# A vision transformer layer with routed experts on one core: end of the attention pipeline, choice of experts and residual traffic rearranged

## The reference

```python
h = einsum('bnd,de->bne', patches(x), W)                  # 768 -> 192
h = h + attention(layernorm(h))                           # 12 heads of 16, causal over 36 tokens
logits = layernorm(h) @ router_w.T                        # 8 experts
probs = softmax(logits); top_w, top_i = top_k(probs, 2); top_w /= top_w.sum()
for e in range(8):
    out += w_e * (gelu(flat @ w1[e] + b1[e]) @ w2[e] + b2[e])   # 192 -> 768 -> 192
h = h + out
```

## Time and profile before

| | |
|---|---|
| median of 3 runs | 444.54 us (441.53 to 458.2) |
| profiled execution | 444.34 us |
| its span | 442.4 us |
| mean granted TensorE clock | 0.903 |
| instructions | 14569 |

### The profile page before, as it was taken

How to read it: one execution, slowest core, us unless ns; L and a number is a source line. 1 busy time by engine, 2 the same in 40 slices (tenths; PEclk the granted TensorE clock), 3 DMA queues, 4 the chain that set the end, 5 groups by cost and what they waited for, 6 DMA issues and landing times.

```text
span 442.4 us, 14569 instructions
## 1 busy us (share of the span) xinstructions
PE 354.8 (80%) x5602; PEld 329.0 (74%) x5602; DVE 253.1 (57%) x638; ACT 219.8 (50%) x451; POOL 194.4 (44%) x236
## 2 busy tenths in 40 slices
PE   2788879998989899987622279799899898999920
PEld 2687779888989889877512169799899898999920
DVE  2566447787787766765349734455455455455417
ACT  3555648778888687753411024344344444344400
POOL 9005433446756664332630144465455455454220
PEclk9899999999999999975555579999999999999985
DMA  8757001444432333311006026621111111122039
GB/s 310 212 153 225 3 17 23 122 124 121 120 111 52 98 92 110 107 46 43 3 2 167 5 51 192 218 64 57 46 57 55 55 57 55 48 57 56 28 140 368
DMA packets 28654, 42.81 MB, mean 97 GB/s; under 512 B 12261, under 2 KB 18901, under 8 KB 28461
## 3 DMA queue, kind: packets, MB, share of 16 engines
q1 hardware_dynamic: 24460, 33.37, 25.0%
q0 software_dynamic: 4128, 8.50, 6.6%
HBM read 30.23 MB, written 9.67 MB: 90 GB/s over the span
## 4 chain that ended last, share of the span: by engine, by line
PE 45%; DVE 15%; issue 14%; POOL 10%; ACT 8%; DMA 6%; SPq 1%; POOLq 0%; DVEq 0%; ACTq 0%
PE PSA L1177 16%; PE PSA L1192 13%; PE PSA L958 4%; POOL XF L438 3%; POOL YP L450 2%; DMA REG<-xrows,KBR 2%; DMA W2l<-wqkv 2%; PE PSA L1015 2%; DVE H L947 2%; DVE REG L652 2%; PE PSA L1196 2%; PE PSA L1144 2%; DVE PTR L880 1%; PE PSA L990 1%; PE PSA L1041 1%
## 5 line engine op out<-in xcount | busy, mean ns | idle before, releaser
L1177 PE MATMUL PSA<-YT,W1h 128*128 128x128 f16 x774 | 79.4, 221 | 6.4 <-issue 4.7
L1177 PE MATMUL PSA<-YT,W1l 128*128 128x128 f16 (+1 forms) x516 | 76.6, 222 | 0.0
L482 POOL DMA_INDIRECT yrows<-KBR x43 | 43.9, 1022 | 69.0 <-DVE KBR L924 68.7
L1177 PEld LDWEIGHTS PSA<-YT,W1h 128*128 x774 | 64.6, 99 | 10.8 <-issue 5.5
L1192 PE MATMUL PSA<-W2h,PTR 128*128 x516 | 71.0, 246 | 0.3 <-DVE PTR L652 0.3
L638 ACT ACTIVATE PTR<-PSA 128x768 f32<-128x768 f32 x43 | 34.9, 811 | 69.3 <-PE PSA L1177 69.3
L1192 PE MATMUL PSA<-W2l,PTR 128*128 x258 | 63.5, 246 | 0.0
L477 POOL DMA_INDIRECT REG<-xrows,KBR x43 | 42.5, 987 | 43.0 <-DVE KBR L901 25.3
L643 ACT ACTIVATE PTR<-PTR 128x768 f16<-128x768 f32 x43 | 36.3, 843 | 46.2 <-PE PSA L1196 46.1
L652 DVE SCALAR_TENSOR_TENSOR PTR<-PTR 128x768 f16<-128x768 f32 x43 | 41.2, 958 | 25.9 <-ACT PTR L643 25.9
L958 PE MATMUL PSA<-W2h,REG 128*108 128x192 f16 x396 | 39.2, 261 | 17.7 <-DVE REG L652 17.6
(11 more groups left out here) (163 smaller groups left out, 794.6 us busy)
## 6 DMA issues: line engine op xcount, KB each, us to landing
WSTG<-w SPq DMA_DIRECT2D x16, 384.0 KB, 3.8
WSTG<-w SPq DMA_DIRECT2D x16, 336.0 KB, 3.2
REG<-xt SPq DMA_DIRECT2D x12, 324.0 KB, 4.5
W1l<-xt SPq DMA_DIRECT2D x10, 324.0 KB, 3.4
VB<-VP SPq DMA_DIRECT2D x99, 19.1 KB
hrows<-H SPq DMA_DIRECT2D x1, 1782.0 KB
H<-hrows SPq DMA_DIRECT2D x1, 1728.0 KB, 8.0
xrows<-REG SPq DMA_DIRECT2D x1, 1600.5 KB
```

The costliest lines, as they stand in the source:

```text
L482: gp.indirect_dma_start(out=yrows, out_offset=bass.IndirectOffsetOnAxis(ap=TARGET[:, s:s + 1], axis=0), in_=YO[s % 2], in_offset=None).the ...
L1177: ins = nc.tensor.matmul(bank(2 * u + f // (FC // 2), 128, FC // 2 * ST_)[:, w:w + ST_], weights[a, c], YT[0:rows, at:at + ST_], start=k = ...
```

## The change

- The loop of steps ends at step 21. What is left is written out by hand on each engine: tiles 16 to 21 use PSUM banks 0 and 1 for their transposes and 4 and 5 for their logits, and the projections of tiles 20 and 21 banks 2 and 3.
- The rows and low halves of the second norm of tiles 20 and 21, and the low half of y of tile 21, move from POOL to DVE. The second norm's variances are now computed for tiles 0-3, 4-7, 8-11, 12-15, 16-18, 19, 20 and 21.
- The experts are chosen for tiles 0-3, 4-7, 8-11, 12-15, 16-18 and 19-21 apart. The first three groups stand at the ends of steps b + 5 to b + 9 of DVE, where b is the tile behind the group; the other three stand in the drain. A running sum over tiles (`PASSED_BY`) replaces 40 of the 43 counting products.
- The weight pieces start four steps earlier (`AHEAD = 4`), that is at step -4.
- The expert of each expert tile is computed behind the 0/1 matrices, and these are cut into parts of 16, 12, 10 and 6 columns and not of 11 each.
- `xrows` and `hrows` are each written in two parts, tiles 0-15 and 16-21, and the residual is read back in six pieces of three tokens per partition, behind the gated tiles 4, 7, 10, 13, 16 and 19.

```diff
+        AHEAD = 4
+
         def pieces(i):
-            return range(max(0, 3 * i // 2), min(2 * PIECES, 3 * (i + 1) // 2))
+            return range(max(0, 3 * (i + AHEAD) // 2), max(0, min(2 * PIECES, 3 * (i + AHEAD + 1) // 2)))
+        OWN_BANKS, ON_DVE = 16, 20
+        SECOND_NORMS = [(0, 4), (4, 8), (8, 12), (12, 16), (16, 19), (19, 20), (20, 21), (21, 22)]
+        ROUTED = [(0, 4), (4, 8), (8, 12), (12, 16), (16, 19), (19, 22)]
...
-        PARTS = [(a, a + TOPK * NT // 4) for a in range(0, TOPK * NT, TOPK * NT // 4)]
+        PARTS = [(0, 16), (16, 28), (28, 38), (38, TOPK * NT)]
...
# SP
+            store_residual(0, OWN_BANKS)
             sp.wait_ge(w_lo, 2 * PIECES)
...
+            sp.wait_ge(gates, 4 * ROUTED.index((12, 16)) + 4)
+            store_normed(0, OWN_BANKS)
...
+            sp.wait_ge(gates, 4 * len(ROUTED))
+            store_normed(OWN_BANKS, NT)
+            store_residual(OWN_BANKS, NT)
+            sp.wait_ge(h_stored, 16 * 2)
+            for at in range(0, B * T // 128, 3):
+                sp.wait_ge(y_done, 4 + at)
+                sp.dma_start(HS[:, at * C:(at + 3) * C], hrows[...][:, at * C:(at + 3) * C]).then_inc(h_in, 16)
...
# DVE, end of step(i)
+                for g, (a, b) in enumerate(ROUTED):
+                    if b < OWN_BANKS:
+                        if i == b + 5:
+                            first_max(g)
+                        elif i == b + 6:
+                            first_place(g)
+                        elif i == b + 7:
+                            second_max(g)
+                        elif i == b + 8:
+                            second_place(g)
+                            passed_by(g)
+                        elif i == b + 9:
+                            gate_values(g)
...
# DVE, the drain, in this order (g12, g16, g19: the groups that begin at tiles 12, 16, 19)
+            first_max(g12); residual(20); stats2(20); variances(group(20))
+            outputs(21); late_y_low(21); refine(group(20)); late_norm2_row(20)
+            first_place(g12); logits(16); late_norm2_low(20)
+            residual(21); stats2(21); variances(group(21)); logits(17); second_max(g12)
+            refine(group(21)); late_norm2_row(21); logits(18); second_place(g12)
+            late_norm2_low(21); passed_by(g12); first_max(g16); first_place(g16)
+            logits(19); gate_values(g12); second_max(g16); logits(20)
+            second_place(g16); passed_by(g16); logits(21)
+            first_max(g19); first_place(g19); second_max(g19); second_place(g19); passed_by(g19)
+            gate_values(g16); gate_values(g19)
...
# ACT, the drain
+            inverse_deviation(group(20)); y_hi(21); norm2_out(16); norm2_hi(19); y_out(21)
+            norm2_out(17); norm2_hi(20); norm2_out(18); inverse_deviation(group(21))
+            norm2_out(19); norm2_hi(21); gap(g12); norm2_out(20); norm2_out(21); gap(g16); gap(g19)
...
# PE, the drain
+            project(20); outputs(21); norm2_transpose(NT, 16); transpose_y(21); norm2_transpose(NT, 17)
+            router(NT, 16); project(21); router(NT, 17); norm2_transpose(NT, 18); norm2_transpose(NT, 19)
+            router(NT, 18); norm2_transpose(NT, 20); router(NT, 19); router(NT, 20)
+            norm2_transpose(NT, 21); router(NT, 21)
...
-            for t in range(NT):
-                ins = nc.tensor.matmul(bank(7, ST_, E), ONES, CHOSEN[:, t * E:(t + 1) * E], ...)
+            nc.tensor.matmul(bank(7, ST_, E), ONES, PASSED_BY[:, NT * E:(NT + 1) * E], start=True, stop=True)
-            for d in range(1, NT):
-                ins = nc.tensor.matmul(bank(6, TT, NT * E)[:, d * E:NT * E], ONES[:, 0:TT], CHOSEN[:, 0:(NT - d) * E], ...)
+            nc.tensor.matmul(bank(6, TT, NT * E), ONES[:, 0:TT], PASSED_BY[:, 0:NT * E], start=False, stop=True)
```

425 lines of the change are left out of this document (297 added, 128 removed).

## The result

| | changed kernel | kernel before, on the same chip |
|---|---|---|
| median | 449.59 us (446.77 to 452.78, 4 executions) | 451.37 us (441.53 to 458.63, 4 executions) |
| ratio of the compared executions | 1.015 (1.010 to 1.021) | |
| profiled execution, its span | 451.1, 449.2 us | 444.34, 442.4 us |
| mean granted TensorE clock | 0.881 | 0.903 |

I had said 445.0, from 439.5 to 449.5. The ratio compares executions that lie near each kernel's fastest; before's slower ones dropped out of it, while the changed kernel's four lie close together and all count. By the ratio the changed kernel is 1.5% slower, by the medians 0.4% faster. That already says where to look: before's four times spread over 3.9%, the changed kernel's over 1.3%, and with so few executions neither number is firm.

A forecast was written before the change was run, and what follows sets the result against it. PE bounds pipeline and experts; between them, a POOL, ACT and DVE chain. Terms 3.2 + 0.3 + 0 - 1.1 - 0.6 - 1.3 = +0.5 on 444.34 gave 444.8, with 0.2 for the median 445.0 us; range 439.5 to 449.5.

The forecast's parts named there:

- C: Steps 19 to 21: without their weight pieces, POOL's low half of y ends earlier; -0.95 us, clock fall left in place.
- rival 2: Clock falls in the embedding, 1.6 us once or twice; small drain instructions cost 2.8 more; 449.4 us, chance 0.12.
- B: Pipeline: choices on DVE fit where it waits, and step 13's late `shift` is wanted only later; 0 us, bounds 0 and 2.
- A: Embedding: weight pieces four steps earlier delay the next patches in steps -4, -3 and -2; +3.2 us, bounds 0 and 4.8.
- The pipeline's +0.3 for the low half of y: Pipeline: pairs of larger pieces begin at step 8, stretching POOL's low half of y once more; bounds 0 and 1.0.
- rival 3: Pipeline: choices on DVE hold up POOL's norms, 0.2 us in each of 13 steps, 2.6 us; 447.6 us, chance 0.08.
- D: Drain: DVE becomes the bound, 93 small instructions at 0.20 us; counting begins 1.1 us earlier, C included; bounds -3.9 and +1.7.
- rival 4: Drain shorter, 0.17 us per small instruction: 442.2 us; chance 0.15, alone or with the pieces hidden in the embedding.
- DVE over 90% busy: Sign for the drain: DVE this busy from 210 to 233 us, counting starting at 232.9 less the embedding's shift.
- E: Counting and table: the expert tiles' three instructions leave the path, 1.0 earlier, with +0.4 behind the matrices; -0.6 us.
- F: Expert tiles: residual written before the table and read in six pieces, so PE's wait for a gather goes; -1.3 us.
- rival 5: Expert tiles: the residual's reads still collide, so F does nothing; 446.3 us, chance 0.06.

The follow-up runs named there:

- the repeat: The changed kernel run again with no edit: 444.24 us (440.5 to 457.97, 13 executions), ratio 0.996 to the kernel before.
- the run with fillers: The changed kernel with unread identity products on PE in the pipeline's longest waits (steps 6, 10, 14, 18; 8, 12, 16): 442.28 us, ratio 0.999.
- the kernels with fillers: The changed kernel and the kernel before, each with unread products in PE's pipeline waits: means of 442.7 and 444.8 us over 18 executions each.
- the experiment: The changed kernel with the first three groups' choices moved from the pipeline to the start of the drain on VectorE: 449.0 us, ratio 1.011.

## Why the prediction was wrong, step by step

**The step that failed: the clock.** Under C stands "The clock falls to 1.2 GHz before 193 us. I leave it there", and rival 2 let it fall once or twice more, in the embedding only, for 1.6 us together. I took the pipeline's full clock as given because the one profile had it so. In its place: three falls in the pipeline with 31 us at 1.2 GHz. Of the 13.4 us that nineteen steps lost, they are 12; the rest is the choices' 1.0 (under B) and 0.2 for y. The rows for it were in front of me: PE waits 1.35 us twice and 1.30 once in that pipeline, and the time of the kernel before varied from 441.53 to 458.2 in three runs, 3.8%, which I passed over. A spread of that size in a kernel on one core had a cause, and its profile was of a good execution. No profile of the changed kernel has a pipeline without a fall, so I take 124.3 us for it (123.3 without choices, and 1.0 for them). Where PE is the bound, 31 us at half rate then cost 12.3, or 0.40 us for each; the other pipelines give 0.40 (41 us cost 16.5 in the second profile of the changed kernel), 0.38 (10 us cost 3.9 with PE kept at work behind the counting) and 0.43 (58 us, 25.0, with the pieces one step earlier on before, its other costs included). Which rival was nearest? The second had the right mechanism in the wrong stage, at an eighth of its size. And that the changed kernel's 444.24, in the repeat, lies beside my 445.0 is luck: its work was shorter than my sum, and falls that I had not counted filled the difference.

**A. Pieces in the embedding: +3.2, held.** Without a fall at the start, the changed kernel reaches step 0 at 65.6 and 65.8, before at 62.6, 62.6 and 63.2: +3.0. With the pieces two steps ahead it is 62.6. PE's waits in the embedding, before:

```profile
46.38 1.69 PE L958 MATMUL PSA<-W2h,REG 128*108 128x192 f16 x18 [0.90 <-DVE REG L652]
...
51.20 1.69 PE L958 MATMUL PSA<-W2h,REG 128*108 128x192 f16 x18 [0.91 <-DVE REG L652]
...
57.53 1.69 PE L958 MATMUL PSA<-W2h,REG 128*108 128x192 f16 x18 [1.28 <-DVE REG L652]
```

and after:

```profile
44.65 1.69 PE L1145 MATMUL PSA<-W2h,REG 128*108 128x192 f16 x18 [1.63 <-DVE REG L723]
...
50.92 1.93 PE L1145 MATMUL PSA<-W2h,REG 128*108 128x192 f16 x18 [2.38 <-DVE REG L723]
...
59.23 1.69 PE L1145 MATMUL PSA<-W2h,REG 128*108 128x192 f16 x18 [1.64 <-DVE REG L723]
```

They grew by 0.73, 1.47 and 0.36, where I had 0.8, 1.6 and 0.8. Behind the 2.38 stands the fall of 52 to 56 us. The two profiles differ by 1.7 only, not 3.0, because before's had its fall at 18.6 to 22.0 us, worth 1.3, and the changed kernel's had none there; the changed kernel's own fall at 52 us cost its embedding nothing (65.58 with it, 65.58 without in the run with fillers).

**The pipeline's +0.3 for the low half of y:** 123.3 against 123.1 without a fall, +0.2.

**B. Choices in the pipeline: +1.0, and not 0.** In most steps the choices are free, as I had said. With the full clock in both, the changed kernel and the one with its choices moved out take the same time in steps 11 and 12, which hold three and eight instructions of a choice (6.21 and 6.98 us), and in steps 9 and 10 (13.80) and 17 and 18 (13.3) the sum of two is the same. Steps 13 and 14 are not: 8.21 + 6.52 = 14.73 us with the choices, 6.64 + 7.16 = 13.80 without. Under B stands that step 13's seven instructions make `shift` 1.5 us late and that PE wants its result only later. `shift` did come 1.57 us later, but so did what stands behind it on DVE. The pair of weight pieces of step 14 now falls on POOL's low half of y. With the choices moved out (DVE, POOL, PE; step 13 begins at 149.88):

```profile
159.19 1.61 DVE L725 SCALAR_TENSOR_TENSOR W2l<-WSTG,W2h 128x672 f16<-128x672 f32 x2
160.42 0.79 POOL L491 TENSOR_TENSOR YP<-YF,YP 108x192 f16<-108x192 f32 x1 [1.64 <-ACT YP L622]
161.48 0.35 PE L1262 MATMUL PSA<-IDH,YP 108*96 108x108 f16 x4
```

and with them, in the run with PE kept at work behind the counting, whose pipeline is the changed kernel's (step 13 begins at 148.77):

```profile
159.20 1.61 DVE L723 SCALAR_TENSOR_TENSOR W2l<-WSTG,W2h 128x672 f16<-128x672 f32 x2
159.49 1.73 POOL L491 TENSOR_TENSOR YP<-YF,YP 108x192 f16<-108x192 f32 x1 [1.82 <-ACT YP L622]
161.27 0.39 PE L1257 MATMUL PSA<-IDH,YP 108*96 108x108 f16 x4 [0.74 <-POOL YP L491]
```

Counted from the start of step 13, DVE's pair starts 1.1 us later and POOL only 0.2, so the pair covers all of POOL's work; that takes 1.73 us and not 0.79, and PE waits 0.74. So rival 3 came true once, at 1.0 us, by the large instructions that the choices push about and not by the choices themselves; its 0.2 us in each of 13 steps did not come. The rule that it came from (the Trainium skill, page "SBUF — State Buffer", section "Who interferes with whom": a VectorE instruction with two SBUF inputs locks out a GpSimd one that reads SBUF) agrees with 1.73 against 0.79 here.

This new wait bears on the failed step too. Eight profiled pipelines have it, and six of them have a fall that begins in step 14 or 15, 1.7 to 2.8 us behind its end. Of the ten that don't have it two have a fall there, both with the pieces one step ahead and a wait of 1.58 us in step 14. No run filled this wait alone, so that it causes the fall is likely and not shown.

**C. Steps 19 to 21: -0.95, a little less.** With the clock alike (3 or 4 us at 1.2 GHz in both) it is 14.5 to 13.8, that is -0.7. The -2.5 between the two profiles is mostly the clock: before's fell at 192 us, after's at 212.

**D. The drain: the other term that was mis-sized.** I had -1.1 with C in it, so about 0 for the drain alone; it is -4.1 in the profiles, -3.5 between the kernels with fillers. VectorE's list, first and last, and pieces of it:

```profile
221.81 0.16 DVE L950 TENSOR_SCALAR RT<-RT 108x4 f32<-108x4 f32 x1
...
232.08 0.18 DVE L923 TENSOR_REDUCE RT<-SAME 108x4 f32<-108x32 f32 x1
232.17 0.15 DVE L924 TENSOR_TENSOR RT<-RT 108x4 f32<-108x4 f32 x1
232.36 0.19 DVE L926 TENSOR_TENSOR OH<-EID,RT 108x32 f32<-108x32 f32 x1
232.59 0.19 DVE L929 TENSOR_TENSOR CHOSEN<-OH 108x32 f16<-108x32 f32 x1
...
242.42 0.17 DVE L956 TENSOR_TENSOR REG<-RT,REG 108x3 f32<-108x3 f32 x1
242.53 0.17 DVE L1023 TENSOR_SCALAR KBR<-PSA 128x8 int32<-128x8 f32 x1
```

The list takes 20.7 us where I had 23.3, and its waits are 0.69 where I had 0.6. The large instructions and the waits together are 4.6, start to start, where I had 4.65. So the 93 small ones take 16.1: **0.173 each and not 0.20**. The rows show why: 232.17 starts 0.09 behind its predecessor, on which it doesn't depend; 232.36 starts 0.19 behind and 232.59 0.23, and these wait for theirs. Independent instructions pair up at 0.07 to 0.1 (in each `variances`, each `logits`, and where one chain hands over to another), and interleaved chains have many such places. I had named 0.17 as a bound, and rival 4 for it, but took the rate of one unbroken chain for an interleaved list. The chains moved in by the experiment, longer and unbroken, cost 0.186 each, between the two. The rest, 1.5 us, lies ahead of the list: it begins 5.9 us behind the shift of step 21, 7.44 before, which I put down to the piece of 0.85 us that is gone and to the clock, which fell later. DVE had 0.69 us idle in 20.7, so "DVE over 90% busy" held, and no hand-made order was late.

**E. Counting and table: -0.6;** measured -0.7 in every profile.

**F. Residual: -1.3;** measured -1.1 here and -1.2 or more alone on the kernel before. Over all profiles the stretch takes 172.5 to 173.9 us with the new traffic and 174.0 to 176.5 with the old, so -1.1 may be on the low side. SP in the changed kernel:

```profile
216.90 0.39 SPq L418 DMA_DIRECT2D hrows<-H  x1
...
243.61 1.17 SPq L418 DMA_DIRECT2D hrows<-H  x1
287.17 34.38 SPq L441 DMA_DIRECT2D H<-hrows  x4
```

Nothing is written when the first tile is gated, and PE's last wait for gathered rows is 0.80 us at 264.35; the reads don't collide (rival 5 out).

**The sum.** Without the clock: +3.0 + 0.2 + 1.0 - 0.7 - 3.5 - 0.7 - 1.1 = -1.8 us; the executions with fillers point to -0.8 to -1.4. I had +0.5 for the work. With the clock it is +6.8 between the two spans, and other pairs of executions lie elsewhere.

**What stays open.** Whether the changed kernel's clock falls more often than that of the one before is open: 8 of 17 against 12 of 30 beside it. The weight pieces alone (10 of 14, against 10 of 26) and the two kernels one step ahead (12 of 12) say that the place of the pieces matters. Why a wait of 1.3 us is followed by a fall in one execution and not in the next no run here shows.

## What to carry to other kernels

When the times of a kernel vary by some per cent, look at the granted clock before anything is priced: list PE's waits in the stage where PE is the bound, and ask of every moved piece of work which of them it lengthens, since moving the pieces by one step cost 4% here. Ask too what stands behind the moved work on its own engine: small instructions that fit into idle time in most steps pushed a large one onto another engine's work in one. Test it by unread products in these waits, and judge a change of 1% with and without them. And price a list of small VectorE instructions by its dependences: the full start-to-start time for each that needs its predecessor, half or less for each that does not.

## What the runs showed of the hardware that was not expected

- In a pipeline where PE is busy some 90% of the time, the granted clock fell to 1.2 GHz behind waits of 0.5 to 1.7 us, for 6.8, 6.8 and 17.1 us in one profile, in some executions and not in others with the same waits; twice, both with the pieces one step ahead, it fell (100.4 and 100.1 us) behind waits of only 0.24 and 0.30 us in one step.
- While it is at 1.2 GHz PE has next to no idle time left (8.00 of 8.00 us busy), and in this pipeline the step was later by some 0.4 us for each microsecond at the lower clock (0.38 to 0.43).
- Moving the weight pieces by one step, which lengthened a wait that recurs every fourth step from about 1.3 to 1.6 us, turned times above 449 us from some into all (460.9 us against 444.2; on the kernel before, 468.9 against 445.2).
- Unread products in the waits brought most of that back (447.5 for 460.9), and cost nothing that could be measured on the kernel before (444.9 against 445.2).
